# First group of a GPS layer by halves: statistics, root and normalised rows of two tiles at a time, key weight loaded and split ahead of group 1

## The chip, the cores and the metric

One NeuronCore of a Trainium2 chip runs the whole kernel; the other seven cores are idle. The metric is the device time in microseconds (us) of one execution. Engines are named as in the profile: PE is the matrix engine, DVE the vector engine, ACT the activation engine, POOL GpSimd, SP the engine that only issues transfers (DMAs).

## The reference

The input x has 12500 rows of 256 numbers. What matters here is the very first step of the layer and the two products that follow at once:

```python
xn = _layernorm(x, axis=-1)
xt = jnp.matmul(xn, weight).reshape(-1, heads, out_ch)      # graph part, table that is gathered from
alpha_l = einsum('ehd,hd->eh', xt[row], attn_l); alpha_r = einsum(..., xt[col], attn_r)
k = (xn @ Wk).reshape(N, L, H, D);  K = elu(k) + 1.0         # linear attention
KV = einsum('nshd,nshv->nhdv', K, v);  ... K.sum(axis=1)
x = x + gnn(xn) + mix(xn)
x = x + ffn(_layernorm(x, axis=-1))
```

Keys and the table of xt are needed of all rows before any row can be finished, since the attention sums over all rows and the graph part gathers arbitrary rows. That makes two passes over the rows.

## The kernel before

Rows are worked on in 25 groups: 24 of 512 rows (four tiles of 128) and a last one of 212 rows. Phase 1 goes over all groups and makes the normalised rows, the keys, the sum of keys times rows, and the tables in memory; phase 2 goes over them again and makes the output. The matrix products are made of three float32r products each (high by high, low by high, high by low part: `split_mm`, L272 to L274), so each operand is split into a high part (a copy with rounding) and a low part (a subtraction).

Each engine has its instructions written out in order by hand, and they meet through semaphores. One group v of phase 1 passes:

- SP loads x into `xb` (`load_x`, two transfers: 112 rows and 16 rows, L295 and L296).
- DVE: `p1_stats` makes mean and variance of each row (BATCH_NORM_STATS2 at L1211, BATCH_NORM_AGGREGATE at L1216), for the whole group, and raises `mv_x1`.
- POOL: `rstd` makes the reciprocal root as a power of -0.5 (L1776 to L1783, the power at L1779) and raises `rs_x1`.
- ACT: `normalize` writes the normalised tiles `xn1`, one instruction per tile (L915).
- PE transposes them into PSUM; ACT copies that as `x1T_hi`; DVE subtracts for `x1T_lo`.
- PE: `p1_k` multiplies by the key weight `wk`, `p1_table` by the graph weight `wx`, in two pairs of tiles; ACT makes the exponential `kf` and copies the table rows `xts`; DVE finishes `kf`, splits it (`k_hi`), and POOL makes `k_lo` and `xr_lo`; `p1_kx` of PE sums keys times rows.

Two stages of a group run ahead: while PE works on group v, the rows of group v + 1 are already normalised and the statistics of group v + 2 are made. The first two groups are therefore written out by hand ahead of the loop. In that start the first group is already halved in part: x of group 0 arrives in two halves (`x_first`, `x0`), the transposes, `x1T_hi` (L958) and `x1T_lo` (L1268) are made by halves, and PE's `first_k` multiplies the two halves. Statistics, root and normalising of group 0 are one piece each. The DVE goes on with the statistics of group 1, the split of the key weight (`wk_hi` at L1262, `wk_lo` at L1264), the two `x1T_lo`, and then the preparation of the graph weight (`attn_prod` at L1271 to `wx_lo` at L1280), on which `p1_table` of group 0 waits through `w_split1`; then the loop body `phase1(0, 0)` follows (`xr_hi` at L1242, statistics of group 2, `kf` at L1247 and L1249, `x1T_lo` of group 1 at L1233). The second `p1_k` of PE waits for that last one.

The functions and blocks that the diff touches:

Of the kernel before, what the change touches and what calls it, by code (L numbers as in the profile page):

```python
# [9 lines left out]
ALU = mybir.AluOpType  # L10
ACT = mybir.ActivationFunctionType
# [33 lines left out]
for _name, _chunks, _cols in (("Wq", 2, 256), ("W1", 4, 512), ("W2", 4, 256), ("sW1", 2, 256), ("sW2", 2, 128),  # L45
# [9 lines left out]
    "p1_dve", "p1_pe", "p1_pool", "q", "q_den", "q_exp", "q_min", "q_mm", "qz", "qz_hi", "rs_m", "rs_x1", "rs_y",  # L55
# [4 lines left out]
)  # L60
FIRST_LOADS, LATER_LOADS = 3, 27
# [2 lines left out]
def gps_layer(nc, A):  # L64

    ctx = ExitStack()
    with ctx:
        used = [0]

        def sb(name, shape, dt=F32, stack=ctx, side=None):  # L70

            lines = -(-4 * math.prod(shape[1:]) // LINE)
            if side is not None and used[0] % 2 != side:
                stack.enter_context(nc.sbuf_tensor(name + "_side", [P, LINE // 4], F32))
                used[0] += 1
            made = stack.enter_context(nc.sbuf_tensor(name, shape, dt))
            if -(-4 * math.prod(shape[1:]) // HALF_LINE) % 2:
                stack.enter_context(nc.sbuf_tensor(name + "_fill", [P, HALF_LINE // 4], F32))
            used[0] += lines
            return made  # L80

        S = {name: ctx.enter_context(nc.semaphore("s_" + name)) for name in SEMAPHORES}

        def tiles(g):

            return LAST_T if isinstance(g, int) and g == NG - 1 else T

        def nodes(g):
            return LAST_R if isinstance(g, int) and g == NG - 1 else R
# [8 lines left out]
        def due(count):  # L98

            return not isinstance(count, int) or count > 0  # L100
# [10 lines left out]
        def group_of(rows, g):  # L111
            return rows[1] if nodes(g) == LAST_R else rows[0][g]
# [7 lines left out]
        def flat(t):  # L120
            return t[:].rearrange("p j n -> p (j n)")
# [21 lines left out]
        neg_half = sb("neg_half", [R, T])  # L143
        eps = sb("eps", [R, T])
# [3 lines left out]
        rn1 = [sb(f"rn1_{n}", [R, 2, T]) for n in range(2)]  # L148
        rn2 = [sb(f"rn2_{n}", [R, 2, T]) for n in range(2)]
        xb = [sb(f"xb{n}", [R, T, C]) for n in range(2)]  # L150
        bn = [sb(f"bn_{n}", [R, T, 6]) for n in "xmyz"]
        mv = [sb(f"mv_{n}", [R, T, 2]) for n in "xmyzv"]
        rs = [sb(f"rs_{n}", [R, T]) for n in "xmyzv"]
        nm = [sb(f"nm_{n}", [R, T]) for n in "xmyzv"]
        veps = [sb(f"veps_{n}", [R, T]) for n in "xmyzv"]
        nmean = [sb(f"nmean_{n}", [R, T]) for n in "xmyzv"]
        LX, LM, LY, LZ = (0, 4), 1, 2, 3
# [5 lines left out]
        wk_raw = sb("wk_raw", [P, CK, C], stack=ctx0)  # L163
# [20 lines left out]
        x1T_hi = [sb(f"x1T_hi{n}", [P, CK, GR], F32R, stack=ctx1, side=HELD) for n in range(2)]  # L184
# [11 lines left out]
        xn1 = [sb(f"xn1_{n}", [R, T, C], stack=ctx1) for n in range(2)]  # L196
        xr_hi = [sb(f"xr_hi{n}", [R, T, KX_PITCH], F32R, stack=ctx1, side=MOVING) for n in range(2)]
# [15 lines left out]
        xmid = [sb(f"xmid{n}", [R, T, C]) for n in range(2)]  # L213
# [36 lines left out]
        def colT(b, n=None, t=T):  # L250

            return psum[:, b, 0:t * R] if n is None else psum[:, b:b + n, 0:t * R]
# [39 lines left out]
        def in_two(dma, out, in_, sem, rows=R):  # L292

            at = (rows - 1) // 16 * 16
            dma.dma_start(out[0:at], in_[0:at]).then_inc(S[sem], 16)  # L295
            dma.dma_start(out[at:rows], in_[at:rows]).then_inc(S[sem], 16)  # L296
# [10 lines left out]
        def rows_of(name):  # L307
            return A[name].rearrange("(c p) n -> p c n", p=P)
# [15 lines left out]
        def _(sp):  # L324
            def load_x(v, par, prefix):
                in_two(sp, flat(xb[par])[:, 0:tiles(v) * C], group_of(x_rows, v), f"{prefix}{par}", nodes(v))
# [14 lines left out]
            for half, sem in enumerate(("x_first", "x0")):  # L341
                cols = slice(2 * half * C, 2 * (half + 1) * C)
                in_two(sp, flat(xb[0])[:, cols], group_of(x_rows, 0)[:, cols], sem)
            load_x(1, 1, "x")
            sp.dma_start(wk_raw[:], rows_of("L0_mix_Wk")).then_inc(S["wk"], 16)
            sp.dma_start(wx_raw[:, :, 0:C], rows_of("L0_gnn_weight")).then_inc(S["w_first"], 16)
            sp.dma_start(attn_bc[:, 0, :], A["L0_gnn_attn_r"].rearrange("h d -> (h d)").partition_broadcast(P)).then_inc(
                S["w_first"], 16)
# [562 lines left out]
        def _(act):  # L911
# [6 lines left out]
            def p1_norm(v, par):  # L918
                act.wait_ge(S["rs_x1"], v + 1)
                if due(v - 1):  # L920
                    act.wait_ge(S["x1t"], v - 1)
                if due(v - 1):
                    act.wait_ge(S["x_split"], v - 1)
                normalize(xn1[par], lambda j: xb[par][:, j, :], LX[par], "xn1", tiles(v))
# [27 lines left out]
                if more >= 2:  # L952
                    p1_norm(v + 2, par)

            p1_norm(0, 0)
            for half, (of, done) in enumerate((("x1t_first", "x1T_hi_first"), ("x1t", "x1T_hi"))):
                act.wait_ge(S[of], 1)
                act.activation(x1T_hi[0][:, :, 2 * half * R:2 * (half + 1) * R], colT(4 * half, 2, 2),  # L958
# [6 lines left out]
            for v in range(NG - 3, NG):  # L965
                phase1(v, v % 2, more=NG - 1 - v)
                if v == NG - 2:
                    act.wait_ge(S["w2_mean"], 1)
                    for k in range(4):
                        act.activation(wslice(w_hi, "W2", k), wslice(w_raw, "W2", k), ACT.Identity,  # L970
                                       bias=w2_nmean[:, k:k + 1])
                if v == NG - 1:
                    for c in range(CK):
                        act.activation(wslice(w_hi, "W1", 2 + c), wslice(w_raw, "W1", 2 + c), ACT.Identity,
                                       scale=g1_col[:, c:c + 1])
# [230 lines left out]
        def _(dve):  # L1206
            tt, ts, stt = dve.tensor_tensor, dve.tensor_scalar, dve.scalar_tensor_tensor

            def stats(which, tiles, src):
                for j in tiles:  # L1210
                    dve.bn_stats(bn[which % 4][:, j, :], src(j))  # L1211

            def aggregate(which, done):
                dve.drain()
                for j in range(T):
                    last = dve.bn_aggr(mv[which][:, j, :], bn[which % 4][:, j, :])  # L1216
                last.then_inc(S[done], 1)


            def p1_stats(v, par):  # L1220
                dve.drain()
                if due(2 * dma16(v, par)):
                    dve.wait_ge(S[f"x{par}"], 2 * dma16(v, par))
                if due(v - 1):
                    dve.wait_ge(S["rs_x1"], v - 1)
                stats(LX[par], range(tiles(v)), lambda j: xb[par][:, j, :])
                aggregate(LX[par], "mv_x1")
# [26 lines left out]

            dve.wait_ge(S["x_first"], 32)
            stats(LX[0], (0, 1), lambda j: xb[0][:, j, :])
            dve.wait_ge(S["x0"], 32)
            stats(LX[0], (2, 3), lambda j: xb[0][:, j, :])
            aggregate(LX[0], "mv_x1")
            p1_stats(1, 1)  # L1260
            dve.wait_ge(S["wk"], 16)
            dve.tensor_copy(wk_hi[:], wk_raw[:])  # L1262
            dve.drain()
# [1 line left out]
            for half, (of, done) in enumerate((("x1T_hi_first", "x1T_first"), ("x1T_hi", "x1T"))):  # L1265
                part = slice(2 * half * R, 2 * (half + 1) * R)
                dve.wait_ge(S[of], 1)
                tt(x1T_lo[0][:, :, part], colT(4 * half, 2, 2), x1T_hi[0][:, :, part], ALU.subtract).then_inc(S[done], 1)  # L1268
            dve.wait_ge(S["w_first"], 16 * FIRST_LOADS)
            for s in range(2):  # L1270
                tt(attn_prod[:, s, :, :], wx_raw[:, :, 0:C],  # L1271
# [90 lines left out]
            for q in range(CK):  # L1362
                at = kden[:, q, :].rearrange("p (d n) -> p d n", n=MIX_HEADS)[:, :, q * per:(q + 1) * per]
                last = ts(at, head_mask[:, 0:P:MIX_CH].unsqueeze(1).broadcast_to([P, QUAD // MIX_HEADS, per]),
                          kx[:, q, C:C + 1], None, ALU.mult)
# [403 lines left out]
        def _(pool):  # L1769
            ptt, pts = pool.tensor_tensor, pool.tensor_scalar  # L1770

            def rstd(which, mvs, count, done, plus_one=None):

                if due(count):
                    pool.wait_ge(S[mvs], count)
                ptt(veps[which][:], mv[which][:, :, 1], eps[:], ALU.add)  # L1776
                pts(nmean[which][:], mv[which][:, :, 0], -1.0, None, ALU.mult)
                pool.drain()
                ptt(rs[which][:], veps[which][:], neg_half[:], ALU.pow)  # L1779
                pool.drain()  # L1780
                if plus_one is not None:
                    pts(plus_one, rs[which][:], 1.0, None, ALU.add)
                ptt(nm[which][:], nmean[which][:], rs[which][:], ALU.mult).then_inc(S[done], 1)  # L1783
# [4 lines left out]
            pool.drain()  # L1788
            pool.affine_select(out=ident[:], in_=ident[:], compare_op=ALU.not_equal, fill=1.0, base=0,
                               pattern=[[-1, P]], channel_multiplier=1).then_inc(S["ident"], 1)  # L1790
            rstd(LX[0], "mv_x1", 1, "rs_x1", plus_one=rn1[0][:, 0, :])
            pool.memset(gate_w[:], 0.0)
            pool.memset(ob_raw[0:QUAD, :], 0.0)
            pool.memset(out_bias[:].bitcast(F32), 0.0).then_inc(S["zeroed"], 1)
            for n in range(2):
                pool.memset(xr_hi[n][:, :, C:C + 1].bitcast(F32), 1.0)
                pool.memset(xr_hi[n][:, :, C + 1:C + 2].bitcast(F32), 0.0)
                last = pool.memset(xr_lo[n][:, :, C:C + 2].bitcast(F32), 0.0)
# [28 lines left out]
            for n, sign in ((0, 1), (1, -1)):  # L1827
                last = pool.affine_select(out=beats[:, :, n, :], in_=beats[:, :, n, :], compare_op=ALU.is_gt, fill=0.0,
                                          base=0, pattern=[[sign, EXPERTS], [-sign, EXPERTS]], channel_multiplier=0)
# [111 lines left out]
```

## Time and profile before

| what | value |
|---|---|
| median of 3 runs | 1323.7 us |
| the three runs | 1323.70, 1326.29, 1323.53 us |
| profiled execution, its own time | 1328.16 us |
| its span, first to last instruction | 1326.4 us |
| PE busy | 1294.6 us, 98% of the span |
| DVE busy | 1077.4 us, 81% |
| ACT busy | 731.6 us, 55% |
| POOL busy | 666.7 us, 50% |
| granted PE clock, mean | 0.997 |

The profiled execution took 1328.16 us, of which 1.8 us lie around its span; it is 4.5 us above the median of the three runs. Busy PE is modelled from pipelined matmuls, so 98% says that PE hardly ever stands without work, not that it is at its peak.

### The profile page before, as it was taken

To read this page: it belongs to the slowest core of one execution; us is meant where nothing else is said; L and a number is where in the kernel's file an instruction comes from. 1 tells how busy PE (TensorE), PEld (TensorE's weight loads), DVE (VectorE), ACT (ScalarE), POOL (GpSimd) and SP (SyncE) were. 2 spreads that over 40 slices of the span, in tenths; PEclk is the share of its full clock that TensorE was granted. 3 is DMA by queue.
4 is the path that set the end of the run, shared out by engine and by line. 5 is a ranking of instruction groups with operands and counts; after the bars stand their busy time and mean duration, and the time that the engine had idled before them with its cause. 6 is when DMAs were issued, how large, how long until landed. Compare 5 with 4: busy or idle time off the path is not lost.

```text
span 1326.4 us, 26270 instructions
## 1 busy us (share of the span) xinstructions
PE 1294.6 (98%) x8812; PEld 1121.4 (85%) x8812; DVE 1077.4 (81%) x2641; ACT 731.6 (55%) x1332; POOL 666.7 (50%) x771
## 2 busy tenths in 40 slices
PE   6999999898999999999999999999999999999998
PEld 6999999776888888888888888888888888888886
DVE  6888777978888888888888888888878888888875
ACT  4555555334645655555645655555645655555654
POOL 5777777746444453444444453444544453444421
PEclk9999999999999999999999999999999999999999
DMA  6787767522122221222121220222121220212000
GB/s 208 241 287 246 254 222 235 153 60 74 40 66 57 80 77 27 72 64 80 39 64 56 80 80 24 74 62 80 41 63 56 80 80 24 76 60 71 25 17 24
DMA packets 65460, 123.24 MB, mean 93 GB/s; under 512 B 31725, under 2 KB 36176, under 8 KB 65422
## 3 DMA queue, kind: packets, MB, share of 16 engines
q1 hardware_dynamic: 57422, 109.25, 25.5%
q0 software_dynamic: 8000, 13.53, 4.6%
q8 instruction: 19, 0.31, 0.1%
q14 instruction: 19, 0.16, 0.0%
HBM read 70.41 MB, written 52.32 MB: 93 GB/s over the span
## 4 chain that ended last, share of the span: by engine, by line
PE 88%; DVE 4%; issue 3%; ACT 2%; POOL 1%; POOLq 1%; DVEq 1%; ACTq 0%
PE psum L272 26%; PE psum L273 25%; PE psum L274 25%; PE psum L484 5%; PE psum L676 3%; PE psum L729 1%; PE psum L667 1%; PE psum L566 1%; PE psum L739 1%; PE psum L559 1%; POOLq L1780 1%; DVE s_lo L1516 0%; POOL ag L1842 0%; POOL xg L1840 0%; POOLq L1836 0%
## 5 line engine op out<-in xcount | busy, mean ns | idle before, releaser
L1846 POOL TENSOR_TENSOR h_lo<-relu,h_hi 128x1024 fp32r<-128x1024 f32 (+1 forms) x50 | 118.4, 2369 | 142.1 <-ACT h_hi L998 142.1
L272 PE MATMUL psum<-w_hi,h_hi 128*128 128x256 f32 x588 | 165.7, 282 | 4.9 <-ACT e L1009 3.1
L273 PE MATMUL psum<-w_lo,h_hi 128*128 128x256 f32 x588 | 165.0, 281 | 0.0
L274 PE MATMUL psum<-w_hi,h_lo 128*128 128x256 f32 x588 | 164.9, 281 | 0.0
L1846 POOL TENSOR_TENSOR s_lo<-relu,s_hi 128x512 fp32r<-128x512 f32 x23 | 29.6, 1289 | 206.0 <-ACT s_hi L1099 206.0
L272 PE MATMUL psum<-z_hi,w_hi 128*128 128x512 f32 (+1 forms) x300 | 121.6, 405 | 2.0 <-DVE z_lo L1616 1.1
L272 PE MATMUL psum<-xT_hi,w_hi 128*128 128x512 f32 (+1 forms) x300 | 118.9, 396 | 0.2 <-DVE relu L1556 0.2
L1840 POOL DMA_INDIRECT xg<-table_xt,idx x100 | 100.5, 1005 | 34.9 <-issue 33.2
L272 PEld LDWEIGHTS psum<-w_hi,h_hi 128*128 128x128 f32 x588 | 111.5, 190 | 7.1 <-ACT e L1009 3.3
L997 ACT ACTIVATE relu<-psum,h_bias 128x512 f32<-128x512 f32 (+1 forms) x100 | 67.8, 678 | 88.9 <-PE psum L274 88.8
L273 PE MATMUL psum<-z_lo,w_hi 128*128 128x512 f32 (+1 forms) x300 | 116.6, 389 | 0.0
L273 PE MATMUL psum<-xT_lo,w_hi 128*128 128x512 f32 (+1 forms) x300 | 116.5, 388 | 0.0
L274 PE MATMUL psum<-xT_hi,w_lo 128*128 128x512 f32 (+1 forms) x300 | 116.4, 388 | 0.0
L274 PE MATMUL psum<-z_hi,w_lo 128*128 128x512 f32 (+1 forms) x300 | 116.1, 387 | 0.0
L274 PEld LDWEIGHTS psum<-w_hi,h_lo 128*128 128x128 f32 x588 | 112.7, 192 | 0.0
L273 PEld LDWEIGHTS psum<-w_lo,h_hi 128*128 128x128 f32 x588 | 111.6, 190 | 1.0
L1842 POOL DMA_INDIRECT ag<-table_al,idx x100 | 96.6, 966 | 30.5 <-issue 30.5
L915 ACT ACTIVATE row_n<-psum,nm_m,rs_m 128x256 f32<-128x256 f32 x98 | 47.5, 565 | 111.8 <-POOL nm_m L1783 111.8
L1009 ACT ACTIVATE e<-psum,e_bias 128x512 f32<-128x512 f32 (+1 forms) x100 | 67.7, 680 | 49.6 <-PE psum L274 47.0
L1470 DVE SCALAR_TENSOR_TENSOR base<-xb,rn,b_bc 128x256 f32<-128x256 f32 x98 | 91.7, 975 | 0.2 <-issue 0.2
L1003 ACT ACTIVATE scaleT<-psum 32x128 fp32r<-32x128 f32 x98 | 26.4, 270 | 113.7 <-PE psum L720 112.8
L272 PE MATMUL psum<-mT_hi,w_hi 128*128 128x512 f32 (+1 forms) x200 | 80.1, 400 | 0.8 <-DVE mT_lo L1624 0.8
(275 smaller groups left out, 4255.9 us busy)
## 6 DMA issues: line engine op xcount, KB each, us to landing
xb<-in_x SPq DMA_DIRECT2D x47, 448.0 KB, 3.9
xT_hi_table<-x1T_hi SPq DMA_DIRECT2D x25, 512.0 KB, 2.8
xT_lo_table<-x1T_lo SPq DMA_DIRECT2D x25, 512.0 KB, 3.6
xT_hi<-xT_hi_table SPq DMA_DIRECT2D x25, 512.0 KB, 3.8
xT_lo<-xT_lo_table SPq DMA_DIRECT2D x25, 512.0 KB, 4.8
table_xt<-xts SPq DMA_DIRECT2D x24, 455.0 KB, 3.0
out<-xmid SPq DMA_DIRECT2D x24, 448.0 KB, 2.9
xb<-in_x SPq DMA_DIRECT2D x47, 64.0 KB, 4.1
```

The costliest lines, as they stand in the source:

```text
L272: pe.matmul(out, wh, xh, start=first, stop=False)
L273: pe.matmul(out, wh, xl, start=False, stop=False)
L274: return pe.matmul(out, wl, xh, start=False, stop=last)
L484: last = pe.transpose(psum[:, b + c, j * R:(j + 1) * R], src[:, j, c * P:(c + 1) * P], ident[0:R, 0:R])
L676: last = pe.matmul(psum[m * HEAD_CH:(m + 1) * HEAD_CH, 2 + q, 0:t * R], second_w[:, e, :], e1[:, e, 0:t * R], start=True, stop=True)
L915: act.activation(out[:, j, :], src(j), ACT.Identity, bias=nm[which][:, j:j + 1], scale=rs[which][:, j:j + 1]).then_inc(S[done], 1)
L997: act.activation(out[:, 0:t * R], colT(b, t=t), ACT.Relu, bias=bias)
L1009: act.activation(e1[:, e, 0:t * R], colT(bank, t=t), ACT.Relu, bias=e1_bias[:, e:e + 1]).then_inc(S["e1_relu"], 1)
L1470: last = stt(base[:, j, :], xb[par][:, j, :], rn2[par][:, 0, j:j + 1], b2_bc[:], ALU.mult, ALU.add)
L1840: pool.indirect_dma_start(xg[par][:, j, :], None, table_xt.ap(), bass.IndirectOffsetOnAxis(idx[par][:, 1, j:j + 1], 0)).then_inc(S[f"gath{ ...
L1842: pool.indirect_dma_start(ag[par][:, j, :], None, table_al.ap(), bass.IndirectOffsetOnAxis(idx[par][:, 0, j:j + 1], 0)).then_inc(S[f"gath{ ...
L1846: ptt(out, src, hi, ALU.subtract).then_inc(S[done], 1)
```

## The change

Five edits, all in the start of phase 1, ahead of the loop:

- SP issues the load of the key weight ahead of x of group 1 instead of behind it.
- DVE aggregates the statistics of group 0 in two halves, each as soon as its half of x is there; the first raises the new semaphore `mv_first`, the second `mv_x1`.
- POOL runs its root twice, on two columns each, and raises `rs_first` and `rs_x1`.
- ACT waits for each half's root and normalises two tiles behind each; the number of its instructions is the same.
- DVE makes the statistics of group 1 behind the split of the key weight and behind both `x1T_lo` of group 0, no longer ahead of them.

```diff
@@ SP
+            sp.dma_start(wk_raw[:], rows_of("L0_mix_Wk")).then_inc(S["wk"], 16)
             load_x(1, 1, "x")
-            sp.dma_start(wk_raw[:], rows_of("L0_mix_Wk")).then_inc(S["wk"], 16)
@@ ACT
-            p1_norm(0, 0)
+            for half, ready in enumerate(("rs_first", "rs_x1")):
+                act.wait_ge(S[ready], 1)
+                for j in (2 * half, 2 * half + 1):
+                    act.activation(xn1[0][:, j, :], xb[0][:, j, :], ACT.Identity, bias=nm[LX[0]][:, j:j + 1],
+                                   scale=rs[LX[0]][:, j:j + 1]).then_inc(S["xn1"], 1)
             for half, (of, done) in enumerate((("x1t_first", "x1T_hi_first"), ("x1t", "x1T_hi"))):
                 act.wait_ge(S[of], 1)
@@ DVE
             dve.wait_ge(S["x_first"], 32)
             stats(LX[0], (0, 1), lambda j: xb[0][:, j, :])
+            dve.drain()
+            for j in (0, 1):
+                last = dve.bn_aggr(mv[LX[0]][:, j, :], bn[LX[0] % 4][:, j, :])
+            last.then_inc(S["mv_first"], 1)
             dve.wait_ge(S["x0"], 32)
             stats(LX[0], (2, 3), lambda j: xb[0][:, j, :])
-            aggregate(LX[0], "mv_x1")
-            p1_stats(1, 1)
+            dve.drain()
+            for j in (2, 3):
+                last = dve.bn_aggr(mv[LX[0]][:, j, :], bn[LX[0] % 4][:, j, :])
+            last.then_inc(S["mv_x1"], 1)
             dve.wait_ge(S["wk"], 16)
             dve.tensor_copy(wk_hi[:], wk_raw[:])
...
                 tt(x1T_lo[0][:, :, part], colT(4 * half, 2, 2), x1T_hi[0][:, :, part], ALU.subtract).then_inc(S[done], 1)
+            p1_stats(1, 1)
             dve.wait_ge(S["w_first"], 16 * FIRST_LOADS)
@@ POOL
-            rstd(LX[0], "mv_x1", 1, "rs_x1", plus_one=rn1[0][:, 0, :])
+            for half, (of, done) in enumerate((("mv_first", "rs_first"), ("mv_x1", "rs_x1"))):
+                two = slice(2 * half, 2 * half + 2)
+                pool.wait_ge(S[of], 1)
+                ptt(veps[LX[0]][:, two], mv[LX[0]][:, two, 1], eps[:, two], ALU.add)
+                pts(nmean[LX[0]][:, two], mv[LX[0]][:, two, 0], -1.0, None, ALU.mult)
+                pool.drain()
+                ptt(rs[LX[0]][:, two], veps[LX[0]][:, two], neg_half[:, two], ALU.pow)
+                pool.drain()
+                pts(rn1[0][:, 0, two], rs[LX[0]][:, two], 1.0, None, ALU.add)
+                ptt(nm[LX[0]][:, two], nmean[LX[0]][:, two], rs[LX[0]][:, two], ALU.mult).then_inc(S[done], 1)
```

On DVE the rows from the kernel's start stand so before the change (row by row in the order of the program; a name left of the arrow is written, `bn_x` and `mv_x` hold the statistics of even groups and `mv_v` those of odd ones):

```order
L1211 BN_STATS bn_x<-xb 128x6 x4
L1216 BN_AGGR mv_x<-bn_x 128x2 x4
L1211 BN_STATS bn_x<-xb 128x6 x4
L1216 BN_AGGR mv_v<-bn_x 128x2 x4
L1262 CAST wk_hi<-wk_raw 128x512
L1264 TENSOR_TENSOR wk_lo<-wk_raw,wk_hi 128x512
L1268 TENSOR_TENSOR x1T_lo<-psum,x1T_hi 128x2x256 x2
L1271 TENSOR_TENSOR attn_prod<-wx_raw,attn_bc 128x512 x2
L1275 TENSOR_REDUCE wx_raw<-attn_prod 128x2x4 x2
L1278 CAST wx_hi<-wx_raw 128x2x264
L1280 TENSOR_TENSOR wx_lo<-wx_raw,wx_hi 128x2x264
```

And so with the change (its line numbers are four to eleven higher):

```order
L1215 BN_STATS bn_x<-xb 128x6 x2
L1263 BN_AGGR mv_x<-bn_x 128x2 x2
L1215 BN_STATS bn_x<-xb 128x6 x2
L1269 BN_AGGR mv_x<-bn_x 128x2 x2
L1272 CAST wk_hi<-wk_raw 128x512
L1274 TENSOR_TENSOR wk_lo<-wk_raw,wk_hi 128x512
L1278 TENSOR_TENSOR x1T_lo<-psum,x1T_hi 128x2x256 x2
L1215 BN_STATS bn_x<-xb 128x6 x4
L1220 BN_AGGR mv_v<-bn_x 128x2 x4
L1282 TENSOR_TENSOR attn_prod<-wx_raw,attn_bc 128x512 x2
L1286 TENSOR_REDUCE wx_raw<-attn_prod 128x2x4 x2
```

The pair of rows that writes `mv_v` (group 1) went from ahead of `wk_hi` to between `x1T_lo` and `attn_prod`.

On SP the issues at the kernel's start differ in one place, the difference being:

```order
-L295 DMA xb<-in_x 112x1024
-L296 DMA xb<-in_x 16x1024
-L345 DMA wk_raw<-in_L_mix_Wk 128x2x256
+L344 DMA wk_raw<-in_L_mix_Wk 128x2x256
+L295 DMA xb<-in_x 112x1024
+L296 DMA xb<-in_x 16x1024
```

One issue moved up by two; x of group 1 is issued one issue later, and everything behind keeps its place.

## Rows read from the trace of the kernel before

**Rows 1.** Stretches: us, busy (count) of PE, PEld, DVE, ACT, POOL; granted clock; DMA

```profile
10.00:15.00 5.00, 4.39 (x21) 3.74 (x20) 4.51 (x8) 3.66 (x8) 2.04 (x5) 1.00 0.64 226
...
70.00:80.00 10.00, 10.00 (x87) 10.00 (x87) 8.53 (x14) 5.89 (x12) 7.68 (x8) 1.00 0.87 284
```

**Rows 2.** Timeline of PE: start us, length us, instruction [idle before it, releaser]

```profile
11.86 0.55 PE L272 MATMUL psum<-wk_hi,x1T_hi 128*128 128x256 f32 x1 [0.61 <-DVE x1T_lo L1268]
...
17.12 1.49 PE L484 MATMUL psum<-ident,xn 128*128 128x128 f32 x8
18.36 0.37 PE L272 MATMUL psum<-wx_hi,x1T_hi 128*128 128x264 f32 x1
...
20.83 0.39 PE L272 MATMUL psum<-wx_hi,x1T_hi 128*128 128x264 f32 x1 [0.76 <-ACT xts L951]
...
22.56 0.38 PE L272 MATMUL psum<-wk_hi,x1T_hi 128*128 128x256 f32 x1
...
25.50 1.03 PE L484 MATMUL psum<-ident,xn 128*128 128x128 f32 x8
...
325.97 0.58 PE L272 MATMUL psum<-w_hi,h_hi 128*128 128x256 f32 x1 [3.10 <-ACT e L1009]
```

**Rows 3.** Timeline of DVE, 3 to 23 us

```profile
3.58 0.75 DVE L1211 BATCH_NORM_STATS2 bn_x<-xb 128x6 f32<-128x256 f32 x2 [3.58 <-DMA xb<-in_x]
4.96 0.75 DVE L1211 BATCH_NORM_STATS2 bn_x<-xb 128x6 f32<-128x256 f32 x2 [0.63 <-DMA xb<-in_x]
5.79 0.38 DVE L1216 BATCH_NORM_AGGREGATE mv_x<-bn_x 128x2 f32<-128x6 f32 x4
7.95 1.41 DVE L1211 BATCH_NORM_STATS2 bn_x<-xb 128x6 f32<-128x256 f32 x4 [1.78 <-DMA xb<-in_x]
9.72 0.40 DVE L1262 CAST wk_hi<-wk_raw 128x512 fp32r<-128x512 f32 x1
...
11.92 0.69 DVE L1268 TENSOR_TENSOR x1T_lo<-psum,x1T_hi 128x512 fp32r<-128x512 f32 x1 [0.20 <-ACT x1T_hi L958]
12.53 1.28 DVE L1271 TENSOR_TENSOR attn_prod<-wx_raw,attn_bc 128x512 f32<-128x512 f32 x2
...
16.38 0.69 DVE L1242 CAST xr_hi<-xn 128x1024 fp32r<-128x1024 f32 x1
...
19.00 1.07 DVE L1247 TENSOR_SCALAR kf<-kf 128x1024 f32<-128x1024 f32 x1
...
21.29 1.22 DVE L1233 TENSOR_TENSOR x1T_lo<-psum,x1T_hi 128x1024 fp32r<-128x1024 f32 x1
```

**Rows 4.** Timeline of POOL, the roots of groups 0 and 1

```profile
6.25 0.20 POOL L1776 TENSOR_TENSOR veps_x<-mv_x,eps 128x4 f32<-128x4 f32 x1 [4.58 <-DVE mv_x L1216]
...
6.79 1.04 POOL L1779 TENSOR_TENSOR rs_x<-veps_x,neg_half 128x4 f32<-128x4 f32 x1
...
8.20 0.20 POOL L1783 TENSOR_TENSOR rn<-nmean_x,rs_x 128x4 f32<-128x4 f32 x1
...
9.89 0.29 POOL L1776 TENSOR_TENSOR veps_v<-mv_v,eps 128x4 f32<-128x4 f32 x1 [0.69 <-DVE mv_v L1216]
...
12.15 0.20 POOL L1783 TENSOR_TENSOR rn<-nmean_v,rs_v 128x4 f32<-128x4 f32 x1
```

**Rows 5.** Timeline of ACT, 8 to 19 us

```profile
8.43 2.08 ACT L915 ACTIVATE xn<-xb,rn,rs_x 128x256 f32<-128x256 f32 x4 [6.33 <-POOL rn L1783]
...
18.65 1.03 ACT L933 ACTIVATE x1T_hi<-psum 128x1024 fp32r<-128x1024 f32 x1 [0.26 <-PE psum L484]
```

**Rows 6.** Transfers of the first 9 us: count, KB, us from issue to landing

```profile
wk_raw<-in_L_mix_Wk SPq DMA_DIRECT2D x1, 256.0 KB, 4.8
...
xb<-in_x SPq DMA_DIRECT2D x1, 64.0 KB, 4.8
```

**Rows 7.** Busy time and granted clock around 325 us: PE busy, clock, DMA share, GB/s

```profile
326.00:330.00 4.00, 4.00 (x19) 0.50 0.04 7
...
332.00:333.00 1.00, 1.00 (x6) 0.97 0.00 0
```

2 rows, old and new, of the table SEMAPHORES are left out of this document.

## The prediction

> **What bounds the kernel now.** I read the page's busy shares first, then PE's waits, then the start engine by engine. PE is busy for 98% of the span, and its list of waits holds none at all between 22.4 and 218 us; a stretch from the loop of phase 1 shows it without a gap, 10.00 of 10.00 us busy [rows 1]. So from the second `p1_k` on, at 22.56 us [rows 2], phase 1 is as long as PE's work. The change touches nothing behind that point. It is worth what it does to the moment at which that product starts, one for one, plus what it does to PE's clock.
>
> What ends last ahead of 22.56 is DVE's `x1T_lo` of group 1, 21.29 + 1.22 = 22.51 us [rows 3]. Followed back, DVE has work without a real gap from `attn_prod` at 12.53 on; the reader should see that each row of DVE there starts where the one before ends. Ahead of it stands a relay in which each engine waits for another: x of the second half lands at 4.96, statistics and aggregates end at 6.17 [rows 3], POOL's root takes 6.25 to 8.40 [rows 4], ACT's four tiles 8.43 to 10.51 [rows 5], and through PE, ACT and DVE the second `x1T_lo` starts at 11.92 [rows 3]. While the relay runs DVE is free, and it uses that: the statistics of group 1 (1.78 us of idle ahead of them, for their x) and the key weight's split both lie there.
>
> **The change, part by part.** I price it at the start of that second `x1T_lo`, then along DVE.
>
> *The halves.* The statistics of tiles 0 and 1 end at 3.58 + 0.75 = 4.33; with two aggregates (four took 0.38) `mv_first` is there at about 4.65, POOL starts at 4.7. The second half's aggregates end at about 6.0. Both root passes run on POOL one behind the other. Call the length of one P. The second starts at 4.7 + P (or at 6.1, if that is later) and ends P later. ACT then needs 0.03 plus two tiles, 1.08 us (half of 2.08, and the overlap), and from the end of the last tile to the second `x1T_lo` it is 11.92 - 10.51 = 1.41 us, as before: ACT now does both copies behind its last tile again, so the first half's copy gains nothing from its early transposes. The second `x1T_lo` starts at 4.7 + 2P + 2.52 = 7.22 + 2P.
>
> What is P? With four columns the pass takes 2.15 us, of which the power is 1.04 and the other four instructions and two drains 1.11 [rows 4]. No row shows a power on two columns. Upper bound: as on four, P = 2.15, start 11.52, a gain of 0.40 us. Lower bound: a power at the price of the add of the same size, 0.20, P = 1.31, start 6.1 + 1.31 + 2.52 = 9.93, a gain of 1.99. The small adds and scalings of POOL cost 0.20 to 0.29 for four numbers per partition, so most of such an instruction is not its elements; what the power has above that, 0.84, may be. I take it nearer to the upper end, P = 1.94, start 11.1: gain 0.8 us.
>
> The Trainium skill ("GPSIMD Engine Reference", section 3.1, elementwise cycle accounting) speaks against the halves: it gives such an instruction a dispatch cost and some 2.6 cycles per element, so that two columns fewer save next to nothing. That would be P = 2.15, and the sum below would be +1.6 instead of +1.2. The trace's power, at five times the add of the same size, shows that its elements or its function cost more than that rule says, so it doesn't decide.
>
> *Statistics of group 1.* They leave a gap and enter the chain. Their price in a busy stretch is read from group 2's: `xr_hi` starts at 16.38 and `kf` at 19.00, 2.62 us, less 0.61 for the cast itself, 2.0 us (1.41 of statistics, 0.38 of aggregates, drains) [rows 3]. In DVE's order they now stand ahead of `attn_prod`, `wx_lo`, `xr_hi`, `kf` and `x1T_lo` of group 1: all of them come 2.0 later, less the gain.
>
> *The key weight.* Its load took 4.8 us from issue to landing [rows 6]; issued one place earlier, at 2.66, it is there by 7.5. The split (a cast of 0.40 and a subtraction like that of `x1T_lo`, 0.69) is done by 8.7, and PE wants it at 11.0: nothing gained and nothing lost, since it was done in time before as well. If this cover went, each us of lateness would count in full. x of group 1 moves back by one issue, 0.47 us, and lands at about 8.4; it is now wanted at 11.8. Cost nil, 3.4 us of cover. The other loads keep their places.
>
> *Sum.* +2.0 - 0.8 = **+1.2 us** at `x1T_lo` of group 1, so `p1_k` of group 1 starts at 23.75. Bounds: +1.6 and 0.0.
>
> Is anything later than DVE then? Group 1's mean is there at 13.7. POOL's root, 9.89 to 12.35 before, 2.46 us [rows 4], gives 16.25, ACT's tiles 18.35, the transposes 18.7; `kf`'s exponential follows by 19.4 (DVE asks at 20.2), `x1T_hi` of group 1 by 20.4 (DVE asks at 22.5). `p1_table` starts at 18.8 (18.36 before) rather than at `wx_lo`'s end, 17.65; its first pair ends at 20.3, ACT's copies at 21.1, the second pair at 22.7. That is 1.0 us ahead of 23.75: PE's lateness is covered, if its clock is up.
>
> Made against the profiled execution, 1328.16 becomes 1329.4 and its span 1327.6. That execution is 4.5 us above the median of the three runs; a part of this is seen: after a wait of 3.10 us PE's clock was granted at 0.50 from about 325.3 to 332 us [rows 2, 7], which costs half of 6.7, 3.4 us, and the three plain runs lie over 2.8 us too. Against the median, 1323.7 + 1.2 = **1324.9 us**.
>
> **The rivals.**
>
> *A: PE stays at its lower clock (chance 0.33).* In the start PE worked at the lower rate, whatever the granted 1.00 of that stretch says [rows 1]: 24 products of 256 columns took 11.86 to 17.12, 0.219 us each, that is 1.2 GHz; the same 24 from 22.56 to 25.50 took 0.122, that is 2.4 GHz [rows 2]. The rise came between 17.12 and 18.36, after more than 5.3 us of work with no gap. In the changed kernel the block of `first_k` is as long, but behind it PE gets transposes at ACT's pace (0.52 us per tile instead of 0.31), a gap of some 0.9 us between the table's pairs, and one of 1.0 ahead of `p1_k`. If the rise isn't over by then, or the clock falls in this stretch, the table's pairs take 12 x 0.22 = 2.6 us each: the second ends at 24.8 and pushes `p1_k` to 24.9, +2.3; then the lower rate goes on for a while (it lasted 6.7 us at 325 us [rows 7]; some of it is over by then, I take 2 to 5 us), 1 to 2.5 us more. Together +3.3 to +4.8, about 1327.7 us. For it: PE did fall to 0.50 after one wait of 3.10 us [rows 2, 7]. Against it: no single gap here is that long, and the block of 5.3 us alone may lift it. It decides when more than 1.0 us of PE's work is added between 16.5 and 23.75.
>
> The Trainium skill ("TensorE: Matmul & The Clock Gate", section on HAM oscillation) says that an engine fed with gaps between its products drops back to half rate and pays for the way up each time. By that alone this rival would be the forecast, 1327.7; the 0.76 us gap at 20.83 that left the rate up [rows 2] speaks for a milder reading.
>
> *B: the halves pay for the move (0.07).* If the power costs by the element or less, P is at 1.31 to 1.5 and the sum is 0 to +0.3: 1323.8. It decides at P = 1.31, where POOL's first pass ends with the second half's arrival. The rows neither show nor exclude it.
>
> *C: the fall of the clock at 325 us goes away (0.06), the side of faster.* It hangs on one wait of 3.10 us for ACT at 322.9. If the runs of before behind the median hold it and a shifted start spares the changed kernel, 3.4 us come back: 1.2 - 3.4, 1321.5; with P below 1.5 as well, 1320.5. It decides only if the clock stays up there whole. Against it: the stretch between is the same instructions in the same order, only later.
>
> **How the numbers follow.** The forecast, +0.8 to +1.6, has 0.54; its own range is 1323.5 to 1326.0, with half a us for the measurement. About 0.2% (2.6 us) is what a measurement of this kernel can tell from no change. Slower by more: three quarters of A, 0.25. Faster by more: half of C, 0.03. The rest, 0.72, is within. The range takes in B at its lower end and A up to 1328.0, and leaves out C and A's worst: 1322.8 to 1328.0.
>
> **What would show it.** In the changed trace: POOL's power on 128x2 against 1.04; the second pass directly behind the first; ACT's third tile at about 8.6; the second `x1T_lo` at about 11.1; statistics of group 1 at 11.8 with no wait for x; `xr_hi` at 17.6; `x1T_lo` of group 1 ending at 23.7 and `p1_k` behind it. Products 0.12 us apart in both table pairs speak against A, 0.22 for it. The forecast is wrong if `p1_k` of group 1 starts before 22.5 or after 24.5, or if PE later waits where it had not.

## The result and the profile after

The changed kernel takes 1328.26 us (median of 12 runs, 1326.48 to 1329.38), the kernel before 1325.93 us (12 runs on the same chip, 1322.97 to 1326.48). The ratio is 1.0023, 95% interval 1.0013 to 1.0033: slower by 1.7 to 4.4 us. Forecast were +1.2 us and 1324.9 us, range 1322.8 to 1328.0. The three runs that the forecast started from had a median of 1323.7; twelve have one 2.2 us higher. So of the 3.4 us between forecast and result 2.2 lie in the starting point and 1.1 in the effect, by the medians. The two medians are 2.3 us apart; the ratio is taken over all runs and puts the difference at 3.0.

The profiled execution of the changed kernel took 1327.81 us, its span is 1326.1 us, 0.3 less than that of before, although its start ends later; the last section says where that came from. I compare stages, therefore, and not spans.

DVE in the changed kernel's timeline, the rows that answer to [rows 3] (start us, length us, instruction, idle before it):

```profile
3.76 0.75 DVE L1215 BATCH_NORM_STATS2 bn_x<-xb 128x6 f32<-128x256 f32 x2 [3.76 <-DMA xb<-in_x]
...
6.97 0.43 DVE L1272 CAST wk_hi<-wk_raw 128x512 fp32r<-128x512 f32 x1 [0.82 <-DMA wk_raw<-in_L_mix_Wk]
7.47 0.69 DVE L1274 TENSOR_TENSOR wk_lo<-wk_raw,wk_hi 128x512 fp32r<-128x512 f32 x1
10.16 0.69 DVE L1278 TENSOR_TENSOR x1T_lo<-psum,x1T_hi 128x512 fp32r<-128x512 f32 x1 [1.99 <-ACT x1T_hi L962]
11.05 0.69 DVE L1278 TENSOR_TENSOR x1T_lo<-psum,x1T_hi 128x512 fp32r<-128x512 f32 x1 [0.20 <-ACT x1T_hi L962]
11.83 1.41 DVE L1215 BATCH_NORM_STATS2 bn_x<-xb 128x6 f32<-128x256 f32 x4
...
17.48 0.68 DVE L1246 CAST xr_hi<-xn 128x1024 fp32r<-128x1024 f32 x1
...
22.39 1.21 DVE L1237 TENSOR_TENSOR x1T_lo<-psum,x1T_hi 128x1024 fp32r<-128x1024 f32 x1
```

The second `x1T_lo` starts at 11.05, 0.87 us earlier than before; the statistics of group 1 stand behind it with no wait for x; and `x1T_lo` of group 1 ends at 22.39 + 1.21 = 23.60, 1.09 later than before. The 1.99 us of idle ahead of the first `x1T_lo` are new: the work that used to fill them is the work that now stands in the chain.

POOL's powers of the two halves and the one of group 1, for [rows 4]:

```profile
4.92 0.20 POOL L1805 TENSOR_TENSOR veps_x<-mv_x,eps 128x2 f32<-128x2 f32 x1 [3.24 <-DVE mv_x L1263]
...
5.47 0.71 POOL L1808 TENSOR_TENSOR rs_x<-veps_x,neg_half 128x2 f32<-128x2 f32 x1
...
7.23 0.74 POOL L1808 TENSOR_TENSOR rs_x<-veps_x,neg_half 128x2 f32<-128x2 f32 x1
...
14.29 0.68 POOL L1788 TENSOR_SCALAR nmean_v<-mv_v 128x4 f32<-128x4 f32 x1
15.12 1.04 POOL L1790 TENSOR_TENSOR rs_v<-veps_v,neg_half 128x4 f32<-128x4 f32 x1
16.32 0.51 POOL L1793 TENSOR_SCALAR rn<-rs_v 128x4 f32<-128x4 f32 x1 [0.16 <-issue]
```

A power on two columns takes 0.71, not 1.04 and not 0.20; a pass takes 4.92 to 6.70, 1.78 us. The root of group 1 now runs while DVE multiplies, reduces and casts. Its first two instructions and the one behind the power took 0.29, 0.22 and 0.23 before and take 0.55, 0.68 and 0.51 now; it ends at 17.0 where I had 16.25. No run isolates DVE's work as the reason.

PE, for [rows 2], and its clock in three stretches (us, busy of PE, PEld, DVE, ACT, POOL, then the granted clock):

```profile
11.00 0.55 PE L272 MATMUL psum<-wk_hi,x1T_hi 128*128 128x256 f32 x1 [0.61 <-DVE x1T_lo L1278]
...
17.78 2.08 PE L484 MATMUL psum<-ident,xn 128*128 128x128 f32 x8 [1.79 <-ACT xn L915]
19.51 0.57 PE L272 MATMUL psum<-wx_hi,x1T_hi 128*128 128x264 f32 x1
...
23.14 0.39 PE L272 MATMUL psum<-wx_hi,x1T_hi 128*128 128x264 f32 x1 [0.76 <-ACT xts L951]
...
24.71 0.28 PE L272 MATMUL psum<-wk_hi,x1T_hi 128*128 128x256 f32 x1
```

```profile
15.00:18.00 3.00, 1.21 (x9) 0.98 (x8) 2.85 (x5) 0.96 (x2) 1.73 (x3) 1.00 0.12 31
18.00:22.00 4.00, 3.95 (x19) 3.32 (x18) 3.68 (x11) 2.93 (x5) 3.61 (x4) 0.59 0.44 130
22.00:25.00 3.00, 2.24 (x18) 2.03 (x17) 2.90 (x4) 0.76 (x4) 1.55 (x4) 0.98 0.19 75
```

The reader is to see four things. PE waits 1.79 us behind `first_k` for the rows of group 1, a wait that was not there before. Then its granted clock is at 0.50 for a stretch (mean 0.59 from 18 to 22 us). The first table pair takes 19.51 to 22.4 instead of 18.36 to 20.1, so that ACT's copies and the second pair end late. And the second `p1_k` starts at 24.71, not at 23.6 when its operand was there. Before it started at 22.56. In phase 1 that distance then stands still: ACT's `kf` of group 1 and that of the last group are both 1.9 us later. They stand so in the changed kernel:

```profile
27.64 1.03 ACT L940 ACTIVATE kf<-psum 128x1024 f32<-128x1024 f32 x1
...
242.82 0.58 ACT L940 ACTIVATE kf<-psum 128x512 f32<-128x512 f32 x1
```

And so before:

```profile
25.70 1.03 ACT L940 ACTIVATE kf<-psum 128x1024 f32<-128x1024 f32 x1 [0.48 <-PE psum L274]
...
240.89 0.58 ACT L940 ACTIVATE kf<-psum 128x512 f32<-128x512 f32 x1
```

Why is the wait behind `first_k` so long? Its rows come late, and PE is early: its products start 0.21 us apart up to 15.2 us and 0.12 apart behind that, so `first_k` ends at 16.0.

### The profile page after: what moved, and what is told of

It reads as the page before. It is cut to its first block, busy times and chain, and to the rows that moved or that the text cites. A ratio compares the mean times of both kernels' runs of the same rounds, so it can differ in the third digit from the quotient of the medians.

```text
span 1326.1 us, 26278 instructions
## 1 busy us (share of the span) xinstructions
PE 1294.6 (98%) x8812; PEld 1120.3 (84%) x8812; DVE 1085.9 (82%) x2641; ACT 731.3 (55%) x1332; POOL 668.8 (50%) x776
## 4 chain that ended last, share of the span: by engine, by line
PE 87%; DVE 4%; issue 3%; ACT 2%; POOL 2%; POOLq 1%; DVEq 1%; ACTq 0%
PE psum L272 25%; PE psum L274 25%; PE psum L273 25%; PE psum L484 5%; PE psum L676 3%; PE psum L729 1%; PE psum L667 1%; PE psum L566 1%; PE psum L739 1%; PE psum L559 1%; POOLq L1791 1%; DVE s_lo L1527 0%; POOL xg L1860 0%; POOL ag L1862 0%; DVE w_lo L1335 0%
```

## The experiments

Each kernel was timed against runs of the kernel before on the same chip, in four sessions (medians of before: 1332.66 us in the first, 1332.53 in the second, 1325.6 in the third, 1328.16 in the fourth). The start can be read to a tenth of a us in a profile; the whole times of before lie 6.5 to 9 us apart within a session. This table has both. The times are us from the span's start; the clock column says when it was granted at 0.50 ahead of 30 us. A start is that of one profiled execution, a ratio that of 12 runs (five for order_only).

| kernel | `first_k` starts | `x1T_lo` of group 1 ends | second `p1_k` | second `kf` of ACT | clock at 0.50 | ratio to before, 95% |
|---|---|---|---|---|---|---|
| before | 11.86 | 22.51 | 22.56 | 25.70 | no | |
| before_again | 11.86 | 22.53 | 22.58 | 25.63 | no | |
| changed | 11.00 | 23.60 | 24.71 | 27.64 | 18.7 to 22.1 | 1.0023 (1.0013 to 1.0033) |
| after_again | 10.90 | 23.51 | 24.09 | 27.02 | 17.4 to 20.8 | 1.0007 (0.9992 to 1.0021) |
| after_look | 11.33 | 23.94 | 26.05 | 29.31 | 19.9 to 26.7 | one run |
| after_third | 11.00 | 23.62 | 23.67 | 26.73 | no | 1.0019 (1.0008 to 1.0030) |
| order_only | 11.98 | 24.58 | 26.67 | 29.97 | 20.6 to 27.4 | 1.0039 (1.0025 to 1.0053) |
| order_only_filled | 11.83 | 24.45 | 24.50 | 27.55 | no | 1.0012 (0.9996 to 1.0028) |
| after_filled | 11.34 | 23.96 | 24.01 | 27.14 | no | 1.0005 (0.9994 to 1.0016) |
| before_double_stats | 11.90 | 24.29 | 24.33 | 27.38 | no | 1.0011 (1.0002 to 1.0019) |
| halves_only | 11.66 | 22.02 | 22.07 | 25.11 | no | 0.9997 (0.9983 to 1.0011) |
| stats_in_gap | 11.31 | 21.68 | 21.73 | 24.77 | no | 0.9988 (0.9977 to 0.9999) |
| stats_in_gap_2 | 11.76 | 22.31 | 22.36 | 25.40 | no | 0.9992 (0.9982 to 1.0001) |
| key_load_by_act | 12.75 | 23.39 | 23.45 | 26.50 | no | 1.0017 (1.0003 to 1.0032) |

**The cost of the move alone.** Before, with the work of a group's statistics once more in the chain:

```diff
                 tt(x1T_lo[0][:, :, part], colT(4 * half, 2, 2), x1T_hi[0][:, :, part], ALU.subtract).then_inc(S[done], 1)
+            stats(LX[1], range(T), lambda j: xn1[0][:, j, :])
+            dve.drain()
+            for j in range(T):
+                dve.bn_aggr(mv[LM][:, j, :], bn[0][:, j, :])
             dve.wait_ge(S["w_first"], 16 * FIRST_LOADS)
```

> The kernel before with four extra statistics and four extra aggregates on DVE between the second x1T_lo of group 0 and attn_prod, into a scratch that is overwritten later; nothing uses them. It has the cost of the move alone, without its late mean of group 1. Chain theory: all of DVE's chain is 1.8 to 2.0 us later, p1_k of group 1 starts at 24.4 to 24.6, PE has no gap behind first_k and its clock stays up; whole time +1.8 to +2.0 against before. Rival (DVE has slack in that chain): the second p1_k is late by less than 1 us. If the hand-over to phase 2 answers a shift of the start with clock falls, the time is above +3.

`x1T_lo` of group 1 ends at 24.29, +1.78, `p1_k` follows at once, the clock stays up. DVE has no slack in that chain: what is put in comes out at `p1_k` in full. One row matters for the clock as well. PE waited 1.83 us here, after dense products and ahead of dense products, and the granted clock was 1.00 throughout:

```profile
24.33 0.38 PE L272 MATMUL psum<-wk_hi,x1T_hi 128*128 128x256 f32 x1 [1.83 <-DVE x1T_lo L1233]
```

**The order alone.** The key weight's load ahead of x of group 1, and `p1_stats(1, 1)` behind both `x1T_lo`, with group 0 in one piece (the loads' edit is left out here):

```diff
             aggregate(LX[0], "mv_x1")
-            p1_stats(1, 1)
...
+            p1_stats(1, 1)
             dve.wait_ge(S["w_first"], 16 * FIRST_LOADS)
```

> The kernel before with the change's order alone: load of the key weight ahead of x of group 1, statistics of group 1 behind both x1T_lo; group 0 stays one piece for statistics, root and normalising. Chain theory: first_k starts at 11.9 as before, x1T_lo of group 1 is 2.0 us later (ends 24.5), the mean of group 1 is late as in the changed kernel, so PE waits behind first_k and its clock may fall there; p1_k starts at 24.6 without a fall, at 25.5 with one: +2.0 to +2.9 in the start. Rival (the halves cause the loss): no more than +0.5 against before.

`x1T_lo` of group 1 ends at 24.58, +2.07, and `p1_k` starts another 2.1 later, with the clock down from 20.6 to 27.4. The direction is as expected and the size is not: `p1_k` is 4.1 us later than before, where 2.9 was the most I had. The rival is out: the order costs, not the halves. The waits of PE from 17 to 27 us in this kernel's timeline:

```profile
18.75 1.83 PE L484 MATMUL psum<-ident,xn 128*128 128x128 f32 x8 [1.37 <-ACT xn L915]
...
23.86 0.59 PE L272 MATMUL psum<-wx_hi,x1T_hi 128*128 128x264 f32 x1 [0.76 <-ACT xts L951]
```

And PE busy, the granted clock and the DMA share of two stretches:

```profile
19.00:22.00 3.00, 2.89 (x16) 0.77 0.28 81
22.00:25.00 3.00, 2.24 (x10) 0.50 0.26 94
```

**The halves alone.** The changed kernel with loads and statistics of group 1 put back (the loads' edit is left out here):

```diff
             last.then_inc(S["mv_x1"], 1)
+            p1_stats(1, 1)
             dve.wait_ge(S["wk"], 16)
...
-            p1_stats(1, 1)
             dve.wait_ge(S["w_first"], 16 * FIRST_LOADS)
```

> The changed kernel with the loads and the statistics of group 1 back in their old places; only the halves of group 0 are left. Chain theory: the relay of group 0 is 0.9 us shorter, but DVE then works on the statistics of group 1 (from 7.95) and the key weight's split until 10.9 and comes to the first x1T_lo no earlier than before, so first_k starts at 11.8 and the second x1T_lo at 11.7 to 11.9: -0.2 to 0.0, p1_k at 22.4 to 22.6, ratio 0.9995 to 1.0003. Rival (the halves give their 0.9 us by themselves): p1_k at 21.7, ratio 0.9993. Rival (the halves cost): p1_k later than 22.9.

`p1_k` at 22.07, 0.5 us ahead of before, between my -0.2 and the rival's -0.8. I had overlooked that with both `x1T_hi` there in time the two `x1T_lo` run back to back:

```profile
7.97 1.41 DVE L1215 BATCH_NORM_STATS2 bn_x<-xb 128x6 f32<-128x256 f32 x4 [1.89 <-DMA xb<-in_x]
...
10.83 1.28 DVE L1279 TENSOR_TENSOR x1T_lo<-psum,x1T_hi 128x512 fp32r<-128x512 f32 x2
12.03 1.28 DVE L1282 TENSOR_TENSOR attn_prod<-wx_raw,attn_bc 128x512 f32<-128x512 f32 x2
```

`attn_prod` starts at 12.03 instead of 12.53 and the whole chain with it. The whole time doesn't resolve that (0.9997).

**Statistics in the idle stretch.** The changed kernel, with one line moved:

```diff
             tt(wk_lo[:], wk_raw[:], wk_hi[:], ALU.subtract).then_inc(S["wk_split"], 1)
+            p1_stats(1, 1)
             for half, (of, done) in enumerate((("x1T_hi_first", "x1T_first"), ("x1T_hi", "x1T"))):
...
-            p1_stats(1, 1)
             dve.wait_ge(S["w_first"], 16 * FIRST_LOADS)
```

> The changed kernel with the statistics of group 1 moved once more: behind the split of the key weight and ahead of both low parts of group 0, where its trace shows DVE idle from 8.2 to 10.2 us. Chain theory (the start lost 1.1 us on DVE, because 2.0 us of statistics stand in the chain, and 0.85 us more because PE's clock fell behind first_k): the statistics of group 1 run from about 8.4 to 10.2, x1T_lo of group 1 ends near 21.7 (22.51 before, 23.60 changed), group 1's rows are normalised in time so that PE has no gap behind first_k, the clock doesn't fall there, and the second p1_k starts near 21.8. Whole time 0.8 us below before, ratio near 0.9994. Rival (any shift of the start sets PE's clock off in the hand-over to phase 2, wherever the start ends): p1_k is early all the same, but the whole time is 1 to 2 us above before.

> The same kernel as stats_in_gap (statistics of group 1 in DVE's idle stretch ahead of the low parts), timed again beside the changed kernel. Chain theory: p1_k at 21.7 again, -0.8 us against before, ratio 0.9988 to 0.9997; 2 to 3 us below the changed kernel.

In the first session:

```profile
8.73 1.41 DVE L1215 BATCH_NORM_STATS2 bn_x<-xb 128x6 f32<-128x256 f32 x4 [0.65 <-DMA xb<-in_x]
10.21 0.38 DVE L1220 BATCH_NORM_AGGREGATE mv_v<-bn_x 128x2 f32<-128x6 f32 x4
10.51 1.25 DVE L1279 TENSOR_TENSOR x1T_lo<-psum,x1T_hi 128x512 fp32r<-128x512 f32 x2
```

`p1_k` at 21.73, 0.83 ahead of before and 2.98 ahead of the changed kernel; the clock stays up. In the second session statistics of group 1 waited for x until 9.18 and ACT was later as well, and `p1_k` came at 22.36, 0.2 ahead and not the 0.8 that I expected. Both ratios are below one (0.9988 and 0.9992, that is 1.6 and 1.1 us). The first interval excludes one by 0.0001 and the second holds it. So the start is 0.2 to 0.8 us earlier, and that the whole kernel is faster than before is likely, but not settled. The rival, that the hand-over to phase 2 takes the gain back, did not come.

**Filling PE's wait.** The changed kernel and order_only, each with products whose results nothing uses, in the place where PE waited (14 of them here, 12 in order_only_filled):

```diff
             first_k(1).then_inc(S["k_mm"], 1)
+            for n in range(14):
+                pe.matmul(psum[:, 6, 0:C], tile(x1T_hi[0], 0, 0), wk_hi[:, 0, :], start=True, stop=True)
             p1_transpose(1, 1)
```

> The changed kernel with 14 extra products on PE between first_k and the transposes of group 1, into a part of PSUM that is overwritten later; their results are used by nothing. They fill the 1.8 us in which PE waits there. Chain theory: the clock stays up, the products of both table pairs are 0.12 us apart (0.22 in the changed kernel's first pair), and the second p1_k starts at 23.7, when x1T_lo of group 1 is there, not at 24.7: 1.0 us below the changed kernel, still 1.1 above before in the start. Rival (the first pair's pace isn't what makes p1_k late, ACT's copies are): p1_k stays at 24.7 and the time that of the changed kernel.

> order_only with 12 extra products on PE behind first_k, in the 1.4 us in which PE waited there for group 1's rows; nothing uses them. In order_only x1T_lo of group 1 was there at 24.6 and the second p1_k started at 26.7, with PE's clock at 0.50 from 20.2 to 27.8. Clock theory: the fall is set off by that wait; filled, the clock stays up, p1_k starts at 24.6 to 24.8, and the second kf of ACT, 29.97 there, comes at 27.7 to 27.9: 2.0 to 2.2 us given back. Rival (the fall comes from the slow pace of the transposes and the rest of the stretch, whatever stands in the wait): p1_k at 26 or later.

Both have the clock up and `p1_k` right behind its operand: 24.01 behind 23.96, 24.50 behind 24.45. The timeline of order_only_filled shows the fill, what is left of the wait, and the start:

```profile
18.61 1.83 PE L484 MATMUL psum<-ident,xn 128*128 128x128 f32 x8 [0.84 <-ACT xn L917]
...
22.67 0.39 PE L272 MATMUL psum<-wx_hi,x1T_hi 128*128 128x264 f32 x1 [0.76 <-ACT xts L953]
24.50 0.39 PE L272 MATMUL psum<-wk_hi,x1T_hi 128*128 128x256 f32 x1
```

The same 0.76 us of waiting between the pairs is there as in order_only, and as before the change; it doesn't bring the clock down. The transposes behind the fill are still at ACT's pace (1.83 us for eight, as in order_only). Against order_only `p1_k` is 2.17 us earlier.

**The changed kernel again.** Three more profiles, two of them with timed runs:

> The changed kernel, unchanged, timed once more. Chain theory: x1T_lo of group 1 ends at 23.6 to 24.0 and the second p1_k starts there if PE's clock stays up, 1 us later if it falls behind first_k; whole time +1.2 to +2.2 against before, ratio 1.0009 to 1.0017. If a part of the loss comes from elsewhere (the hand-over), the ratio is 1.0022 again.

> The changed kernel once more, for one more profile. Clock theory: PE's clock falls to 0.50 behind first_k again, somewhere between 17 and 22 us, and the second p1_k starts 0.5 to 1.1 us behind the end of x1T_lo of group 1; if the fall hangs on chance, some execution has none and p1_k starts at 23.6.

> The changed kernel, timed a third time for the size of the loss. Start theory (1.0 to 1.1 us of DVE's chain, and 0.5 to 2.5 us of PE's clock, by where the fall lies): second kf of ACT at 27.0 to 29.3, against 25.6 to 25.7 before; whole time +1.5 to +3.6, ratio 1.0011 to 1.0027. Rival (the loss is DVE's chain alone and the rest was noise of the first measurement): ratio 1.0008.

The end of `x1T_lo` of group 1 is at 23.5 to 23.9 in all; the fall of the clock cost 0.6, 1.1 and 2.1 us in three executions and nothing in the fourth, after_third, where PE waited 1.32 us for the same rows. The 2.1 of after_look is outside the 0.5 to 1.1 that I expected. These are the rows of after_third:

```profile
17.78 1.83 PE L484 MATMUL psum<-ident,xn 128*128 128x128 f32 x8 [1.32 <-ACT xn L915]
...
23.67 0.39 PE L272 MATMUL psum<-wk_hi,x1T_hi 128*128 128x256 f32 x1
```

And this is the wait in after_again:

```profile
17.68 2.07 PE L484 MATMUL psum<-ident,xn 128*128 128x128 f32 x8 [2.35 <-ACT xn L915]
```

The wait was 2.35, 1.79 and 1.39 us in after_again, changed and after_look, and 1.37 in order_only; the falls cost 0.6, 1.1, 2.1 and 2.1. So a longer wait did not cost more. It is longer where `first_k` came to the higher pace earlier (from 13.8 us on in after_again, 15.2 in changed, only with its last product in after_look), and there the clock fell and came back earlier, too: what counts is how much of PE's work lies in the stretch at 0.50.

So one profile of a filled kernel doesn't show by itself that the fill keeps the clock up. Together it is four falls in the five profiles with that wait unfilled, none in the nine others, of which two are the filled ones. What in that stretch brings the clock down isn't settled. In after_again it fell at 17.4, 2.1 us into the wait and ahead of the transposes. In the three others it fell behind the wait, 0.9 to 1.9 us after the first transposes, which come at ACT's pace. But before_double_stats had a wait of 1.83 us among dense products, the filled kernels had the slow transposes behind a wait of 0.68 and 0.84, after_third had both (1.32 us), and the clock stayed up in all four. Over the four executions of the changed kernel the second `kf` is 1.1, 1.4, 2.0 and 3.6 us later than the mean of before (25.67), 2.0 in the mean. The three ratios, 1.0023, 1.0007 and 1.0019, average 1.0016 or 2.2 us. The ratio of after_third, 1.0019, lies within what I expected of it, although its one profile shows no fall.

**The key weight by another queue.** stats_in_gap with

```diff
-            sp.dma_start(wk_raw[:], rows_of("L0_mix_Wk")).then_inc(S["wk"], 16)
             load_x(1, 1, "x")
...
+            act.dma_start(wk_raw[:], rows_of("L0_mix_Wk")).then_inc(S["wk"], 16)
             for half, ready in enumerate(("rs_first", "rs_x1")):
```

> stats_in_gap with the load of the key weight issued by ACT at its start, so that x of group 1 is issued where it was in the kernel before. In stats_in_gap x of group 1 was awaited until 8.7 and 9.2 while the relay was ready for the low parts at 10.1. Chain theory: x of group 1 lands at 7.9 to 8.2, its statistics are done by 9.9, the first x1T_lo starts at 10.1, x1T_lo of group 1 ends at 21.4 and p1_k starts there: 1.1 us below before, ratio 0.9990 (0.9982 to 0.9996). Rival (the key weight's transfer, now beside x of group 0, makes that later): statistics of group 0 start 0.3 us or more later than 3.7 and the gain is gone.

A miss; the rival holds. x of group 0, the head of the whole relay, is the one that pays:

```profile
5.17 0.75 DVE L1215 BATCH_NORM_STATS2 bn_x<-xb 128x6 f32<-128x256 f32 x2 [5.17 <-DMA xb<-in_x]
```

3.7 became 5.17, and `p1_k` 23.45. SP issued x of group 0 at the same time as ever (0.82 us), and its 224 KB parts took 3.2 us from issue to landing, where they took 2.4 in stats_in_gap. So a load that a free queue issues early can still delay one that is awaited; what they share isn't shown.

**The kernel before again.**

> The kernel before, unchanged, for a profile on the same chip as its neighbours. Chain theory: the second p1_k starts at 22.5 to 22.9 with no fall of PE's clock ahead of it. If the hand-over to phase 2 (last kf to first mT_hi, 32.2 us in the first trace of before, 40 to 41 us in the four experiments so far) belongs to the chip and not to the start, it follows the chip here too and is within 1 us of its neighbour's.

The start is the same to 0.02 us. The hand-over from phase 1 to phase 2 (last `kf` to first `mT_hi` of ACT) took 39.7 us where the first trace had 32.2. Its neighbour on the same chip, after_again, had 34.3, so one chip can show both; the expectation that the hand-over is within 1 us of its neighbour's failed.

## Why the prediction missed, step by step

- *PE is the bound from the second `p1_k` on, one for one.* Right: 1.9 us late there, 1.9 at the last `kf` of phase 1.
- *The halves.* Right in kind, the size nearly: P = 1.94 was taken, 1.78 measured; the gain at the second `x1T_lo` 0.87 against 0.8. ACT does gain nothing from the early transposes. Halving the columns took 0.33 off the power's 1.04, so it does not cost as an add of its size. The Trainium skill ("GPSIMD Engine Reference", section 3.1) would have left it at next to 1.04; the measurement decides, and the page's rate is that of an add.
- *Statistics of group 1, 2.0 us.* Right: +1.78 in before_double_stats, +2.07 in order_only, and 2.0 - 0.9 = 1.1 at the end of `x1T_lo` in the changed kernel (forecast 1.2, measured 1.09).
- *The key weight's load and x of group 1.* Right: split done by 8.2, no wait for x. But "cost nil" priced only that place. It left the stretch from 8.2 to 10.2 idle, in which the statistics fit, as stats_in_gap showed.
- *"PE's lateness is covered, if its clock is up."* This is the step that failed: the sum took its condition as met. It also named no wait behind `first_k`, though its own terms have one: `first_k` from 11.0 for 5.3 us ends at 16.3, and the first tile behind a root at 16.25 is there at 16.8. The root ended 0.75 us later than summed, at 17.0, since three small instructions of POOL took 0.51 to 0.68, and `first_k` ended 0.3 earlier; PE waited 1.79 us. The clock fell in three of four profiles, and `p1_k` came 0.6 to 2.1 us behind its operand. In the fourth it didn't fall and `p1_k` started 0.05 behind `x1T_lo`: the cover itself was there. Rival A had the lower clock with 0.33; by the profiles it was the likelier case, and its price smaller than I had it: +1.4 to +3.6 in all, not +3.3 to +4.8. The block of `first_k` did lift the pace first, or right behind it; it was lost again in the wait (after_again) or behind it, and it was not a rise that failed to come. On this the Trainium skill ("TensorE: Matmul & The Clock Gate", section on HAM oscillation) says that waits between groups of products throw the engine back to half rate, with waits in its example that are longer than those behind `first_k` here. Four of the five profiles with the wait of 1.3 to 2.4 us agree; the 1.83 us of before_double_stats and the 0.76 between the table's pairs do not.
- *Rivals B and C.* P was not at 1.31; B is out. The clock's fall near 325 us is still there in the changed kernel's trace (329 to 332 us); C did not come.
- *The starting point.* The forecast stood on three runs. Their spread of 2.8 us was seen, and explained, and still their median was used as if it were firm. That is the larger part of the miss in us: the time lies 0.3 above the range's top, 1328.0, and the starting point alone moved by 2.2.

What stays open: the first ratio's centre is 3.0 us and the profile's start explains 1.9 of it; the difference is within the interval, and I have not shown that there is a second cause. Nor is it known in how many of the timed runs the clock fell, since only one execution of each set was profiled.

## What to carry to other kernels

Work that is moved off a relay should be moved into an idle stretch of its engine that ends before the relay comes by; put behind the relay it costs its whole length on the next chain, and the shorter relay only leaves a longer hole. When a late operand makes the matrix engine wait just after it has come up to its pace, count the clock as well as the wait: the same lateness cost 0 to 2.1 us more here. A wait of 1.83 us among dense products cost nothing beyond itself. And a change worth a us needs a baseline of more than three runs before its absolute time is forecast.

## What the runs showed of the hardware

- The same program on the same chip differs by 7 us from run to run, and its mean granted clock goes along in part. In the third session three of the 23 runs of before had a mean clock of 1.000 and took 1321.2 to 1321.4 us, three had 0.995 and took 1328.1 to 1328.6. Between them the order is loose: 1321.4 to 1325.8 us at 0.999, 1322.3 to 1325.7 at 0.997.
- The hand-over from phase 1 to phase 2 has two levels in the 14 profiles: 32.2 to 34.3 us in seven, 39.7 to 40.7 in the other seven. The clock was at 0.50 in it for 0 to 6.8 us in the first seven and for 7.0 to 13.7 in the others. Still the time at 0.50 alone doesn't explain it: after_again and before_again had 6.8 and 7.0 us of it, in one stretch (256 to 263 us) and in two (256 to 260 and 270 to 274), and hand-overs of 34.3 and 39.7. What makes the step is open.
- In phase 2 a turn, from one `mT_hi` of ACT to the next, lasts either about 42.45 or about 42.6 us. In the first trace of before 15 of the 21 full turns from the second on were long, in that of the changed kernel two, together 2.2 us. That is how the changed kernel's span came out 0.3 us shorter in spite of its start; why a turn is long is open.
- POOL's scaling on 128x4, 0.22 us in the kernel before, took 0.68 in the changed kernel while DVE ran `attn_prod`, and the one behind the power 0.51, against 0.23, while DVE cast `wx_hi`.
